# Mode products in four 64x64 tiles, and mixed modes turned to rows of kx by VectorE transposes

## What is computed

```python
def _fourier_layer(v, W1, W2):
    x_ft = jnp.fft.rfft2(v)
    out1 = jnp.einsum('bixy,ioxy->boxy', x_ft[:, :, :12, :12], W1)
    out2 = jnp.einsum('bixy,ioxy->boxy', x_ft[:, :, -12:, :12], W2)
    ...
    return jnp.fft.irfft2(out_ft, s=(Sx, Sy))
for i in range(4):
    x1 = _fourier_layer(v, W1, W2)
    x2 = jnp.einsum('bcxy,cd->bdxy', v, w_w[i]) + w_b[i]
    v = batch_norm(x1 + x2)
    if i < 3: v = relu(v)
out = einsum('bcxy,cu->bxyu', v, q_w) + q_b
```

## Time and profile before

| | |
|---|---|
| median of 3 runs | 1611.89 us (1611.37 to 1615.3) |
| profiled execution, its own time | 1598.89 us |
| its span, first to last instruction | 1597.1 us |
| mean granted TensorE clock | 0.892 |
| PE busy / DVE / ACT / POOL | 79% / 51% / 33% / 17% of the span |

### The profile page before, as it was taken

How to read it: one execution, slowest core, us unless ns; L and a number is a source line. 1 busy time by engine, 2 the same in 40 slices (tenths; PEclk the granted TensorE clock), 3 DMA queues, 4 the chain that set the end, 5 groups by cost and what they waited for, 6 DMA issues and landing times.

```text
span 1597.1 us, 40205 instructions
## 1 busy us (share of the span) xinstructions
PE 1263.5 (79%) x18179; PEld 738.9 (46%) x18179; DVE 822.1 (51%) x886; ACT 529.0 (33%) x778; POOL 276.7 (17%) x380
## 2 busy tenths in 40 slices
PE   3489389999959759988995884989999767963587
PEld 3355155555535325555553641554555455222552
DVE  6332257777633226675674332576766622028754
ACT  1133134454423213443443331344434333020140
POOL 5541300220214210102020313002202041210000
PEclk9789679999989869999998896999999989986788
DMA  5479987988619999999991799999999152961001
GB/s 139 105 173 281 232 184 186 228 211 194 150 41 218 278 206 285 327 326 312 304 290 37 177 282 224 289 307 325 303 315 303 39 185 116 335 245 45 1 1 27
DMA packets 194708, 328.52 MB, mean 206 GB/s; under 512 B 33432, under 2 KB 139304, under 8 KB 175588
## 3 DMA queue, kind: packets, MB, share of 16 engines
q1 hardware_dynamic: 180090, 290.15, 63.6%
q0 software_dynamic: 14448, 35.81, 8.9%
HBM read 164.38 MB, written 142.64 MB: 192 GB/s over the span
## 4 chain that ended last, share of the span: by engine, by line
PE 58%; DMA 16%; DVE 9%; SPq 7%; ACT 5%; issue 3%; POOL 0%; DVEq 0%; ACTq 0%
PE ps L1453 13%; PE ps L1489 11%; PE ps L1521 6%; PE ps L1509 6%; PE ps L1384 5%; DMA arena<-mixed_modes 3%; PE ps L1414 3%; SPq L996 3%; PE ps L1478 3%; DMA arena<-half_inverse 2%; PE ps L1393 2%; DMA mixed_modes<-arena 2%; PE ps L1469 2%; DMA inputs<-mixed_modes 2%; ACT arena L1270 2%
## 5 line engine op out<-in xcount | busy, mean ns | idle before, releaser
L1489 PEld LDWEIGHTS ps<-arena 48*128 48x128 f32 x3072 | 191.1, 197 | 120.6 <-issue 80.2
L1489 PE MATMUL ps<-arena 48*128 48x128 f32 x3072 | 211.1, 289 | 39.9 <-DMA arena<-half_inverse 35.2
L941 POOL DMA_DIRECT2D arena<-arena x162 | 95.7, 599 | 816.2 <-ACT arena L1287 815.5
L1270 ACT ACTIVATE arena<-ps,arena 128x1024 f32<-128x1024 f32 x96 | 112.2, 1202 | 245.1 <-PE ps L1489 205.7
L1384 PE MATMUL ps<-arena 64*64 64x64 f32 x2304 | 145.3, 284 | 51.4 <-DMA arena<-arena 51.4
L1384 PEld LDWEIGHTS ps<-arena 64*64 64x64 f32 x2304 | 130.2, 154 | 110.9 <-issue 106.7
L1279 ACT ACTIVATE ps<-ps 128x1024 f32<-128x1024 f32 x144 | 145.5, 1011 | 103.0 <-PE ps L1453 102.7
L1820 DVE STREAM_TRANSPOSE arena<-ps 128x1024 f32<-128x1024 f32 x96 | 177.3, 1930 | 2.6 <-PE ps L1509 2.6
L1453 PE MATMUL ps<-arena 32*32 32x512 f32 x2944 | 160.4, 618 | 7.4 <-issue 6.5
L1521 PE MATMUL ps<-arena 128*64 128x96 f32 x2304 | 124.5, 259 | 36.9 <-DVE arena L1820 29.2
L1509 PE MATMUL ps<-arena 32*32 32x512 f32 x3072 | 149.4, 602 | 5.3 <-DVE arena L1810 3.4
(11 more groups left out here) (298 smaller groups left out, 1313.1 us busy)
## 6 DMA issues: line engine op xcount, KB each, us to landing
arena<-half_inverse SPq DMA_DIRECT2D x96, 384.0 KB, 9.5
half_inverse<-arena SPq DMA_DIRECT2D x66, 512.0 KB, 7.1
maps<-arena SPq DMA_DIRECT2D x112, 256.0 KB, 4.0
maps<-inputs SPq DMA_DIRECT2D x112, 256.0 KB, 6.2
arena<-maps SPq DMA_DIRECT2D x28, 1024.0 KB, 10.2
maps<-arena SPq DMA_DIRECT2D x28, 1024.0 KB, 6.8
inputs<-maps SPq DMA_DIRECT2D x28, 1024.0 KB, 9.5
arena<-in_mode_w POOLq DMA_DIRECT2D x48, 384.0 KB, 6.1
```

What stands on the lines that cost most here:

```text
L1270: nc.scalar.activation(half(h_out(l, q), h)[:, 1024 * pair:1024 * pair + 1024], ps[:, 2 * pair:2 * pair + 2, :].rearrange("p b n -> p (b n ...
L1489: last = nc.tensor.matmul(ps[:, b, at:at + 128], gtile[s][rows, 4 * b + 2 * h + n, :], iy[rows, :], start=False, stop=(i >= 2 and n == 1))
```

## The change

The unit of the mix is no longer one ky but half of the kx of a *pair* of ky (p is the pair, e which of the two, h which half of the 12 kx, u = 2p + h). The output rows of PSUM are then (e, real or imaginary, channel) and its banks are m. For that the 12 calls of a half use all four 64x64 tiles (rows of m, outputs of e).

```diff
-                for k in range(6):
-                    for m in range(2):
-                        bank_k = (turn + m) % 2
-                        kk_ = 6 * bank_k + k
-                        rows = slice(64 * m, 64 * m + 64)
-                        last = nc.tensor.matmul(ps[rows, 2 * s + bank_k, 64 * k:64 * k + 64], w[rows, kk_, :],
-                                                modes[rows, :, t, y, kk_], start=True, stop=True)
+                for k in range(3 * turn, 3 * turn + 3):
+                    for e in range(2):
+                        for m in range(2):
+                            rows = slice(64 * m, 64 * m + 64)
+                            last = nc.tensor.matmul(ps[64 * e:64 * e + 64, 2 * s + m, 64 * k:64 * k + 64],
+                                                    ring[(2 * p + e) % RING][rows, 6 * h + k, :],
+                                                    modes[rows, :, e, p, 6 * h + k], start=True, stop=True)
```

```diff
+            def turn_kx(l, p):
+                if p == 0:
+                    for s in range(2):
+                        link(nc.vector.memset(mixed(l, s)[:, 1536:2048], 0.0))
+                if p >= 2:
+                    dve.wait_ge(ix_full, group_of(l, 4 * (p - 1)))
+                for i in range(2):
+                    j = (i + first_half(l)) % 2
+                    src = mixed(l, p).rearrange("p (k b) -> p b k", b=BATCH)[:, 32 * j:32 * j + 32]
+                    dst = kxin(l, p)[:, 1024 * j:1024 * j + 1024].rearrange("p (b o) -> p b o", o=32)
+                    nc.vector.transpose(dst, src).then_inc(kx_turned, 1)
```

The inverse has again 24 groups of two calls per mix, each now for 16 images and both ky of a pair. It begins behind the seventh half instead of the ninth, so that 6 groups are left at the end, and the norm's sums stand behind all of them:

```diff
+        AHEAD = 6
+            for u in range(KY):
+                for turn in range(2):
+                    steps.append(("half", u, turn))
+                    if 2 * u + turn >= AHEAD and groups:
+                        steps.append(("inverse", groups[0], groups.pop(0) % 2))
+            for n in groups:
+                steps.append(("inverse", n, n % 2))
+            return steps + [("sums", 0, 0), ("norm", 0, 0)]
```

More of the change, by code:

```diff
@@ L100, in shape_tables @@
     real = (p < 32).astype(np.float32)[:, None]
+    lone = np.where(p < 64, -0.25, 0.0).astype(np.float32)[:, None]
     ones = np.ones((128, 1), np.float32)
@@ L860, in slot_use, with mode_of, group_of, first_half @@
             return QUADS // 2 * l + q // 2
-        def mode_of(l, ky):
-            return KY * l + ky
+        def mode_of(l, u):
+            return KY * l + u
+        GROUPED = 4 * KYH
+        def group_of(l, n):
+            return GROUPED * l + n
+        def first_half(l):
+            return ORDER[l][0] // 8
+        def chunk(l, n):
+            return 2 * ((n // 2 + first_half(l)) % 2) + n % 2
+        AHEAD = 6
         def mix_order(l):
-            groups = [(ky, g) for ky in range(KY) for g in range(2)] if l < PASSES else []
+            groups = list(range(GROUPED)) if l < PASSES else []
             steps = []
-            for ky in range(KY):
+            for u in range(KY):
                 for turn in range(2):
[L872 to L897, removed]
+                    steps.append(("half", u, turn))
[4 more added lines that the diff above has]
+            return steps + [("sums", 0, 0), ("norm", 0, 0)]
+        LAST_GROUPS = GROUPED - AHEAD
+        def inverse_bank(n):
+            return 6 if n < LAST_GROUPS else (6, 0, 2)[(n - LAST_GROUPS) % 3]
+        def skip_bank(u):
+            return 6 if u == 1 else 4
+        def half_stored(l, p):
+            return 64 * (KYH // 2 * l + p // 2)
         def staged(l, batch):
@@ L1058, in layer_pass @@
                     sp.wait_ge(map_st[s], stores(l, 0))
-                sp.wait_ge(ix_st[3], half_stored(l, KY - 1) + 32)
+                for j in range(2):
+                    sp.wait_ge(ix_st[2 + j], half_stored(l, KYH - 1) + 64)
                 for i in range(QUADS - KEPT):
@@ L1588, in _ @@
                     pe.wait_ge(pm_ev, 2)
-                    for b in range(2):
-                        last = nc.tensor.matmul(ps[:, 5 + b, 0:384], ix[0:48, :], kx_last[0:48, 384 * b:384 * b + 384],
-                                                start=True, stop=True)
+                    for ri in range(2):
+                        if ri:
+                            pe.wait_ge(xl_real, 1)
+                        rows = slice(32 * ri, 32 * ri + KX)
+                        for b in range(2):
+                            last = nc.tensor.matmul(ps[:, 5 + b, 0:384], ix[rows, :], kx_last[rows, 384 * b:384 * b + 384],
+                                                    start=(ri == 0), stop=(ri == 1))
+                        if ri == 0:
+                            last.then_inc(xl_real, 1)
                     last.then_inc(xl_full, 1)
@@ L1805, in turn_map @@
                 if q == 0 and h == 0:
-                    for ky in (KY - 2, KY - 1):
-                        dve.wait_ge(ix_st[ky % 4], half_stored(l, ky) + 32)
+                    for j in range(2):
+                        dve.wait_ge(ix_st[2 + j], half_stored(l, KYH - 1) + 64)
                 src = half(h_out(l, q), h).rearrange("p (b u y) -> p b u y", u=2, y=32)
```

241 lines of the change are left out of this document (109 added, 132 removed).

## The result

The changed kernel takes **1585.3 us** (median of 4 runs, 1582.5 to 1593.1) against 1611.6 of the kernel before (4 runs, 1601.2 to 1615.3): a ratio of 0.985, 95% interval 0.981 to 0.990, 26 us less. The forecast was 49 less, 1563 with a range of 1536 to 1602. Sign and range held; 23 us of the gain, nearly half, are missing. Its profiled execution is the slowest of its runs (1593.1 us, span 1591.2), that of before is quicker than any of the four (1598.9), so the spans alone differ by only 6 us. The stages say more.

The account below looks back on a forecast made before the run. Bound: mainly PE, with 17.4 us of DRAM waits in the first mix and slow clock behind them. Three mixes from 359 to 315 (44 less), layer 3 7 less, end 1.7 more: 49 off 1611.9, 1563 us; range 1536 to 1602.

Parts of the forecast that it names:

- The waits for DRAM go, products in 0.65 us: Mixes: no wait for modes from DRAM; a half's 24 loads take about 0.65 us on four tiles instead of 1.28.
- A: Rival: tiles on the same rows share the strided reader, products get no faster, 28 us gained, 1591; chance 0.28.
- C: Rival: strided reads of all four tiles take turns, a half's products take 2.54 us, 1640, slower; chance 0.05.
- Transposes of 1.75 us: VectorE's transposes in the mixes: 1024 elements read 256 bytes apart take 1.74 us, 3.5 us a pair.
- Rival B: Transposes run at the dense rate, 0.65 to 0.7 less for each of 12, 8 a mix: 1538; chance 0.1.
- The ring of 13.9 us a pair: Middle of a mix: ACT, DVE and PE wait in a circle, two units of 5.2 plus 3.5 for transposes.
- The clock allowance, 4.2 us a mix: Slow clock behind PE's 3.9 us waits: one inverse 0.95 dearer, four or five times a mix.
- The opening, 25 us: Start of a mix: from its first product until the third inverse group is released, about 25 us.
- The last groups, 5.6 us: Near a mix's end: five of the last six inverse groups until the first half of the images is out.
- the round trip, 14.5 us: End of a mix: four store issues 2.6, landing 4.9, first load 6.9, with the wait for the semaphore.
- Layer 3, 7 less: Layer 3's mix, without inverse or transposes: 4.14 us a ky falls to 3.5 through faster products, 7 us saved.
- The end, 1.7 more: Kernel's end: a second wave of products with its wait, 1.1, and one more issue, 0.65.

Follow-up runs that it names:

- e11: Changed kernel, VectorE's transposes reading 1024 neighbouring elements instead of elements 256 bytes apart (modes wrongly ordered, only times count): 1558.4 us.
- e3: Changed kernel plus twelve products nobody reads, on PE ahead of the inverse groups that wait for the transposes: 1572.6 us.
- e7: e2 with the first pair turned only after the third ky's sums and two sums nobody waits for put later: 1506.0 us, ratio 0.939 to before.
- e6: e2 with half of the stores of the last two image halves issued by ACT instead of SyncE: 1512.0 us, ratio 0.942 to before.
- e2: The late turn: changed kernel with VectorE transposing a pair after its evacuation of the odd inverse group, not before: 1518.6 us, ratio 0.943 to before.
- e4: Changed kernel, products of one parity of ky issued before the other's, meant to let only two of four tiles run side by side: 1598.7 us.
- e9: e7 plus 14 and 38 products nobody reads in PE's idle time at the end of a mix: 1511.3 us, ratio 0.938 to before.

## Why the prediction was right in kind and forecast nearly twice the gain

- **The waits for DRAM go, products in 0.65 us:** right. No wait for mixed_modes is left, and 24 loads take 0.63 to 0.65 us at the high clock, so rivals A and C fall. The measured 1585.3 lies nearer to A's 1591 than to the forecast, but that is a coincidence of the sums: what A says of the products did not happen. Each tile starts a record every 0.11 us and four tiles do so side by side, also two on the same rows. The rule of the Trainium skill ("TensorE: Matmul & The Clock Gate", Part 3) is that a weight load overlaps running matmuls only if it is for other rows. This trace does not agree with it: four loads start every 0.11 us, two for each half of the rows, while products of 0.29 us run on both. That tiles on the same rows would take turns was my own inference from that rule, and it is wrong here.
- **Transposes of 1.75 us:** nearly; 1.90 busy, 3.6 to 3.7 a pair in the chain. Rival B falls, and e11 shows its dense rate as another price: 1.22. The Trainium skill ("Advanced Engine Details and Errata", Memory Cachelines), by which a strided read is slower, agrees.
- **The ring of 13.9 us a pair:** right at the high clock, 14.03 in e3.
- **The clock allowance, 4.2 us a mix: the step that failed first, a term of the sum that was sized too small.** I named the wait of 3.9 us and the slow stretch behind it, then priced one inverse group at 0.95 for four or five of them. But at the low clock PE's work no longer hides: ACT's copy and DVE's sums wait for PE's products and skip, and two inverse groups with two halves of products and skip (8.75 us with the third group) stand in the chain. Four pairs took 62.6 us against 55.7 forecast, 6.9 more, of which 1.6 us a pair goes when the wait is filled (e3). Over the allowance of 4.2 that is 2.7 a mix.
- **The opening, 25 us: 28.0.** The third group was released at 112.21. The fourth unit's skip went on at 16.3 us in place of 14.8; about 1 us of that stands ahead of DVE's first operation (4.1 us in, 3.1 forecast), for which no run gives the cause. That skip had waited 4.6 us, and it and the inverse behind it then cost 1.54 and 2.01 us where 0.8 and 1.06 were forecast: the clock again, in a place where I had put none, and enough for the other 1.5. With the late turn, e7 takes 3 us out of the opening.
- **The last groups, 5.6 us: 6.4,** and **the round trip, 14.5 us: 16.0.** I let the queue of earlier stores go with the modes' stores. In fact the inverse of the last two pairs ends in a burst, and SyncE is 1.9 us late with the first store of the last four and reaches the last of them 3.3 us later, where I had 2.6 for all four; landing then was quicker (3.87 against 4.87), and the load took its 6.5. That adds up to the 1.5, but it does not show that the queue is the cause: in e6, with the late turn, relieving it brought the landing no earlier, and for the changed kernel no run tests it.
- 3.0, 2.7, 0.8 and 1.5 are the 8 us by which the first mix exceeded 105; the other two exceeded it by as much, and three times 8 is 24, about the 23 us missing from 49. About half of the 8 (2.7 and 1.5) is the clock.
- **Layer 3, 7 less:** 8. **The end, 1.7 more:** 4 to 6 between the two traces of each, where the traces of all kernels with the change scatter by 6. **The passes:** not moved by more than they scatter; I took the time of one execution, in which they were short, as their length.
- **The larger omission** is one of reading, not of a term: the chain that I wrote down had the transposes standing between the sums and an evacuation that doesn't need them. The order list put them there. In that place their 3.6 us a pair cost 22 us a mix, 66 in all, more than all that the change gained; behind that evacuation (e2) almost nothing of them is left on the ring. This omission is not what the forecast missed by, since the forecast had the transposes in the same place.

## What to carry to other kernels

When an operation is moved to an engine that stands in a ring of evacuations, ask first what is queued behind it there: put it behind the release that others wait for, where it lies beside their work (here 66 us, for three lines). A wait of TensorE behind which the rows show the low clock is to be priced as the whole stretch behind it, with what that stretch newly puts on the path, not as one instruction that got slower. And a single profiled execution gives the stages that are its own; a stage bound by DMA needs a second trace before its length enters a sum.

## What the runs showed of the hardware

- Four tiles of 64x64 with moving operands 576 bytes apart run side by side, each with a record every 0.11 us, and records of further tiles are started while earlier ones still wait for theirs (20 of 24 loads in 0.65 us in e4 although only two tiles have work at a time by program order).
- A 32x32 block transpose of 128x1024 fp32 takes 1.90 us reading at a stride of 256 bytes and 1.22 us densely.
- TensorE's granted clock was at 0.50 behind waits of 3.5 to 3.7 us (the changed kernel), of 2.33 us (e11) and of 2.27 us (e9), and at 1.00 behind one of 0.9 us (e3). It came back after 3.3 to 6.7 us in the mixes and after 20 us at the start of layer 0's pass (e9), where PE was busy 19.3 of 20.4 us.
- With DMA's share at 0.99 to 1.00 a second issuing queue brought the landing forward by nothing, though the issues were through 1.7 us earlier (e6).
